# First expert layer's head: four buffers for scales, separate PSUM banks, another order on GpSimd and VectorE

## The reference, cut to what matters

```python
x = x + _L0_xattn_ref(_layernorm(x), ctx_1024, ctx_1024, ...)
x = x + _L0_ffn_ref(_layernorm(x), ...)          # below; its x is the normalised one
...
def _L0_ffn_ref(x, g1, be1, mix_w, mix_b, g2, be2, router_w, w1, b1, w2, b2):
    res = x
    n = layer_norm(x, g1, be1)
    x = res + n + (n @ mix_w + mix_b)
    res = x
    n = layer_norm(x, g2, be2)
    probs = softmax(flat @ router_w)              # flat: n as 4096 x 128
    topw, topi = top_k(probs, 2)
    h = silu(einsum('td,edf->tef', flat, w1) + b1)
    y = einsum('tef,efd->ted', h, w2) + b2
    return res + einsum('te,ted->td', combine, y) # combine: topw at the two chosen experts
```

## Time and profile before

| what | value |
|---|---|
| median of 3 runs | 1463.12 us (1462.66 to 1466.3) |
| profiled execution, its own time | 1462.91 us |
| span of the profiled execution | 1461.1 us |
| busy: PE / DVE / ACT / POOL | 80% / 68% / 46% / 37% of the span |
| attention of layer 0 ends | at 223.2 us |
| head of the first expert layer | 223.2 to 322.6 us |
| units of the first expert layer | 322.6 to about 510 us |

### The profile page before, as it was taken

How to read it: one execution, slowest core, us unless ns; L and a number is a source line. 1 busy time by engine, 2 the same in 40 slices (tenths; PEclk the granted TensorE clock), 3 DMA queues, 4 the chain that set the end, 5 groups by cost and what they waited for, 6 DMA issues and landing times. The chain is left out here.

```text
span 1461.1 us, 34924 instructions
## 1 busy us (share of the span) xinstructions
PE 1174.6 (80%) x11141; PEld 920.6 (63%) x11154; DVE 987.4 (68%) x2918; ACT 667.0 (46%) x1423; POOL 538.6 (37%) x590
## 2 busy tenths in 40 slices
PE   4799994349999957789987879999799856499991
PEld 2577773238899825566673456667477655399991
DVE  4689886554533248988984678888487777766552
ACT  2467771115555403445564546666233343144440
POOL 3223303674324166534411242431121125652564
PEclk9999995559999957889998989999799988599996
DMA  7887733012223267435532177564200042133542
GB/s 181 205 217 192 184 93 129 30 56 75 82 91 108 66 158 188 116 101 150 144 84 51 52 170 177 144 160 106 87 1 0 6 147 76 53 120 107 147 144 70
DMA packets 140294, 163.33 MB, mean 112 GB/s; under 512 B 15240, under 2 KB 120734, under 8 KB 133196
## 3 DMA queue, kind: packets, MB, share of 16 engines
q1 hardware_dynamic: 131980, 145.38, 37.0%
q0 software_dynamic: 8192, 16.46, 4.0%
HBM read 111.19 MB, written 50.92 MB: 111 GB/s over the span
## 5 line engine op out<-in xcount | busy, mean ns | idle before, releaser
L604 DVE TENSOR_REDUCE A_neg_max<-A_s_bank 128x4 f32<-128x512 f32 x384 | 254.0, 688 | 54.3 <-PE A_s_bank L747 43.9
L464 ACT ACTIVATE A_probsT<-A_st_bank 128x512 f32<-128x512 f32 x384 | 222.3, 602 | 50.1 <-PE A_st_bank L760 48.7
L747 PE MATMUL A_s_bank<-A_k_stack,A_q_stack 72*128 72x128 bf16 x1536 | 159.0, 230 | 42.5 <-DMA A_q_stack<-q_scratch 22.3
L760 PE MATMUL A_st_bank<-A_q_stack,A_k_stack 128*128 128x128 bf16 x1536 | 153.6, 225 | 7.2 <-DVE A_q_stack L620 6.4
L760 PEld LDWEIGHTS A_st_bank<-A_q_stack,A_k_stack 128*128 128x128 bf16 x1536 | 113.0, 104 | 53.5 <-issue 43.5
L747 PEld LDWEIGHTS A_s_bank<-A_k_stack,A_q_stack 72*128 72x128 bf16 x1536 | 107.2, 102 | 57.3 <-DVE A_neg_max L604 30.0
L772 PE MATMUL A_pv_bank<-A_probsT,A_v_pad 128*32 128x128 f32 x3072 | 127.5, 284 | 1.0 <-issue 1.0
L2065 ACT ACTIVATE E_h<-E_h_bank,w_L_b 128x256 f32<-128x256 f32 x184 | 76.8, 471 | 73.2 <-PE E_h_bank L2165 72.1
L2177 PE MATMUL E_y_bank<-E_w,E_h 128*128 x736 | 90.3, 276 | 2.2 <-ACT E_h L2065 0.9
L2165 PE MATMUL E_h_bank<-E_xT,E_w_u 128*128 128x256 f32 x368 | 89.5, 388 | 0.0
L772 PEld LDWEIGHTS A_pv_bank<-A_probsT,A_v_pad 128*32 128x32 f32 x3072 | 74.2, 111 | 24.2 <-issue 2.7
(11 more groups left out here) (369 smaller groups left out, 2639.7 us busy)
## 6 DMA issues: line engine op xcount, KB each, us to landing
A_q_stack<-q_scratch SPq DMA_DIRECT2D x48, 576.0 KB
A_k_stack<-k_scratch SPq DMA_DIRECT2D x32, 576.0 KB
q_scratch<-A_q_parts SPq DMA_DIRECT2D x48, 192.0 KB
A_k_stack<-k_scratch SPq DMA_DIRECT2D x48, 192.0 KB
E_xe<-slots_in SPq DMA_DIRECT2D x53, 128.0 KB, 2.1
slots_out<-E_ye SPq DMA_DIRECT2D x53, 128.0 KB
A_ctxT<-in_ctxT SPq DMA_DIRECT2D x24, 256.0 KB, 9.3
k_scratch<-A_k_parts SPq DMA_DIRECT2D x32, 192.0 KB
```

Source lines behind the costliest of these rows:

```text
L464: act.activation(probsT[n % 2][:, c * HQ:(c + 1) * HQ, :], st_bank[c % 2][:, :].rearrange("k (a q) -> k a q", a=HQ), ACT.Exp, scale=scale) ...
L604: dve.tensor_reduce(neg_max[:, c * HQ:(c + 1) * HQ], s_bank[c % 2][:, :].rearrange("q (a k) -> q a k", a=HQ), AX.X, ALU.max, negate=True). ...
L747: last = pe.matmul(s_bank[c % 2][:, a * S:(a + 1) * S], q_stack[slot][0:COMBO, h, at:at + S], k_stack[slot][0:COMBO, h, at:at + S], start= ...
L760: last = pe.matmul(dst, k_stack[slot][:, h, at:at + S], q_stack[slot][:, h, at:at + S], start=True, stop=spread)
```

## The change

1. `scale_z`, `rstd_x` and `back` get four buffers (`NR = 4`) where they had two.
2. Banks of the head: `mix` of odd groups goes to `h_bank[0]`, `turn_r` to `x_bank` and `y_bank`, logits and counts to `h_bank[1]`. These banks belong to the units, which begin later; PE gets three waits in unit 0 for it. With that, `mix` waits for `z_added` of two groups before, `turn_z` for `n_copied`, and PE's `mix` of a new chunk no longer waits for `index_done`.
3. GpSimd's list: all four `scale_of_z` stand before the first scatter, and `inverse_deviation(1)` and `(2)` come after 4 scatters of chunk 0 and 8 of chunk 1.
4. VectorE's list: `scale(0)` and `scale(1)` come before the conversion of the bias `mix_b`; `statistics` of the groups 2 and 3 before the first `mix`, of 4 and 5 before `normalise` of chunk 0, of 6 and 7 after it; `normalise` before `add_x1`; both `scale` of the next chunk before `below_max`.
5. `convert_rest` is no block any more: its five conversions are in VectorE's list of the expert layer before the first `mix`, and its barrier is gone.

```diff
-        scale_z = [sb(f"scale_z{i}", [S, RT]) for i in range(2)]
+        scale_z = [sb(f"scale_z{i}", [S, RT]) for i in range(NR)]
...
-        l_bank = m_bank
+        in_head = lambda g: g < 2 * HEAD
+        mixed_bank = lambda g: h_bank[0] if in_head(g) and g % 2 else m_bank
+        rows_bank = lambda g: (x_bank, y_bank)[g % 2] if in_head(g) else t_bank[g % 2]
+        logit_bank = lambda c: h_bank[1] if c < HEAD else m_bank
...
             pool.memset(zeros[:, :], 0.0).then_inc(zeroed, 1)
             scale_of_z(0)
+            scale_of_z(1)
             inverse_deviation(0)
-            scale_of_z(1)
+            scale_of_z(2)
+            scale_of_z(3)
             pool.wait_ge(cleared, 16 * len(PARTS))
-            scatter(0, 0, 8)
+            scatter(0, 0, 4)
             inverse_deviation(1)
-            scatter(0, 8, 2 * RT)
-            scale_of_z(2)
-            scatter(1, 0, 10)
+            scatter(0, 4, 2 * RT)
+            scatter(1, 0, 8)
             inverse_deviation(2)
-            scatter(1, 10, 2 * RT)
-            scale_of_z(3)
+            scatter(1, 8, 2 * RT)
...
+            scale(0)
+            scale(1)
             dve.wait_ge(mix_b_loaded, 48)
...
-            scale(0)
-            scale(1)
+            statistics(2)
+            statistics(3)
+            convert(dve, own)
             for c in range(HEAD):
                 for g in (2 * c, 2 * c + 1):
                     mix(g)
                     statistics_1(g)
+                if c == 0:
+                    statistics(4)
+                    statistics(5)
+                normalise(2 * c)
+                normalise(2 * c + 1)
                 add_x1(2 * c)
                 add_x1(2 * c + 1)
-                statistics(2 * c + 2)
-                normalise(2 * c)
-                normalise(2 * c + 1)
-                statistics(2 * c + 3)
-                below_max(c)
+                if c == 0:
+                    statistics(6)
+                    statistics(7)
                 if c + 1 < HEAD:
                     scale(2 * c + 2)
+                    scale(2 * c + 3)
+                below_max(c)
                 choose_first(c)
                 choose_second(c)
-                if c + 1 < HEAD:
-                    scale(2 * c + 3)
                 locate(c)
...
             def mix(g):
                 if g == 0:
                     pe.wait_ge(mix_done, 2)
-                else:
-                    pe.wait_ge(z_added, g)
-                if g % 2 == 0 and g >= 2:
-                    pe.wait_ge(index_done, g // 2)
+                elif g >= 2:
+                    pe.wait_ge(z_added, g - 1 if in_head(g) else g)
...
                 if c + 1 < HEAD:
                     turn_z(2 * c + 2)
+                    turn_z(2 * c + 3)
+                    mix(2 * c + 2)
                 count(c)
                 if c + 1 < HEAD:
-                    turn_z(2 * c + 3)
-                    mix(2 * c + 2)
                     mix(2 * c + 3)
```

More of the change, by code:

```diff
@@ L1566, in routed_ffn @@
         mv_x = sb("mv_x", [S, NB, 2])
-        scale_z = [sb(f"scale_z{i}", [S, RT]) for i in range(2)]
-        rstd_x = [sb(f"rstd_x{i}", [S, RT]) for i in range(2)]
-        back = [sb(f"back{i}", [S, RT]) for i in range(2)]
+        scale_z = [sb(f"scale_z{i}", [S, RT]) for i in range(NR)]
+        rstd_x = [sb(f"rstd_x{i}", [S, RT]) for i in range(NR)]
+        back = [sb(f"back{i}", [S, RT]) for i in range(NR)]
         z = sb("z", [S, RT, D])
@@ L2042, in copy_r @@
                     act.wait_ge(l_ready, g - 1)
-                act.activation(rT[g % 2][:, :], t_bank[g % 2][:, :], ACT.Identity, scale=g2[:, 0:1], bias=be2[:, 0:1])\
+                act.activation(rT[g % 2][:, :], rows_bank(g)[:, :], ACT.Identity, scale=g2[:, 0:1], bias=be2[:, 0:1])\
                     .then_inc(r_copied, 1)
@@ L2124, in turn_r @@
                 pe.wait_ge(r_done, g + 1)
-                pe.wait_ge(n_copied, g + 1)
+                if not in_head(g):
+                    pe.wait_ge(n_copied, g + 1)
+                elif g >= 2:
+                    pe.wait_ge(r_copied, g - 1)
                 for j in range(GB):
-                    last = pe.transpose(t_bank[g % 2][:, j * S:(j + 1) * S], r[:, g * GB + j, :], core.ident[:, :])
+                    last = pe.transpose(rows_bank(g)[:, j * S:(j + 1) * S], r[:, g * GB + j, :], core.ident[:, :])
                 last.then_inc(r_turned, 1)
@@ L2131, in logits @@
                 pe.wait_ge(r_copied, g + 1)
-                pe.wait_ge(z_added, (g | 1) + 1)
+                if not in_head(g):
+                    pe.wait_ge(z_added, (g | 1) + 1)
+                elif g >= 2:
+                    pe.wait_ge(index_done, g // 2)
                 for j in range(GB):
                     i = g % 2 * GB + j
-                    last = pe.matmul(l_bank[:, i * NE:(i + 1) * NE], rT[g % 2][:, j * S:(j + 1) * S], router_w,
+                    last = pe.matmul(logit_bank(g // 2)[:, i * NE:(i + 1) * NE], rT[g % 2][:, j * S:(j + 1) * S], router_w,
                                      start=True, stop=True)
@@ L2152, in turn_slots @@
                     pe.wait_ge(x_copied, u)
+                else:
+                    pe.wait_ge(r_copied, 2 * HEAD)
                 for j in range(2):
@@ L2973, in load_expert, with convert_rest @@
             sp.dma_start(exp_w1[:, at], ap["L0_exp_w1"].rearrange("d e f -> d (e f)")[:, at]).then_inc(exp_w1_loaded, 16)
-        def convert_rest():
-            with nc.Block() as block:
-                @block.vector
-                def _(dve):
-                    dve.wait_ge(rest_loaded, 16 * len(rest_loads))
-                    dve.tensor_copy(core.earlier[:, :], wide_earlier[:, :])
-                    dve.tensor_copy(core.first_tie[:, :], wide_first_tie[:, :])
-                    dve.tensor_copy(q_w2, q_w2f, saturate=False)
-                    dve.tensor_copy(q_b2h, q_b2f).then_inc(quantised, 1)
-                    dve.wait_ge(quantised, 1)
-                    dve.tensor_copy(q_b2, q_b2h)
+        def convert_rest(dve, own):
+            dve.wait_ge(rest_loaded, 16 * len(rest_loads))
+            own.did(dve.tensor_copy(core.earlier[:, :], wide_earlier[:, :]))
+            own.did(dve.tensor_copy(core.first_tie[:, :], wide_first_tie[:, :]))
+            own.did(dve.tensor_copy(q_w2, q_w2f, saturate=False))
+            own.link(dve.tensor_copy(q_b2h, q_b2f))
+            own.did(dve.tensor_copy(q_b2, q_b2h))
         if 0 in stages:
```

38 lines of the change are left out of this document (20 added, 18 removed).

## The result

| what | before | after |
|---|---|---|
| median of 4 runs each, side by side | 1464.71 us (1462.66 to 1468.12) | 1450.13 us (1447.66 to 1455.78) |
| ratio after / before, 95% interval | | 0.9919 (0.9895 to 0.9944) |
| profiled execution, its own time | 1462.91 us | 1452.55 us |
| VectorE's first instruction behind the attention | 224.19 | 222.67 |
| SP's first load of a unit | 320.52 | 306.90 |

The change is faster by 0.8%, which is 11.9 us of 1464.7 (8.2 to 15.4). The forecast of 1452.2 lies 0.4 from the profiled execution and 2.1 from the median. The head, as the table measures it, is 12.10 shorter where 10.8 was predicted. It is measured from the first instruction behind the attention, because the attention itself, which is the same code, ended 1.52 earlier in this execution.

The account below looks back on a forecast made before the run. GpSimd's scatters, held up mutually with VectorE, bound the units' start. Shorter waits bring the first load from 320.52 to 309.7, gain 10.8: 1462.91 - 10.8 = 1452.1, said 1452.2 us; own range 1451 to 1454, with rivals 1449.5 to 1456.5.

Parts of the forecast that it names:

- Barrier and conversions: Start of the expert layer: it begins 1.40 us earlier, but five conversions on VectorE delay the first mix by about 1.05.
- The banks: Head, chunks 0 and 1: a second bank removes the 1.14 us wait; chunk 1's mixes no longer wait for the index.
- then 2.81: GpSimd, after its wait for chunk 2's mixes: inverse_deviation(2) takes 2.81 us, before the last eight scatters.
- Eight scatters: GpSimd, after the deviation of chunk 2: the last eight scatters take 10.06 us and end at 307.1.
- From the last scatter's end to the load: End of the head: the last scatter's landing and the issue take 2.6 us, so the first load comes at 309.7.
- The remaining wait: GpSimd, before the deviation of chunk 2: it waits 1.7 us for VectorE's mixes, behind table(0) and three weight copies.
- The first rival: GpSimd slower beside VectorE's denser list, scatters 1.29 us each, deviations 2.81: gain 8.6, time 1454.3 us; chance 0.16.
- the prediction's sign of 1.3: GpSimd in the head: the prediction is wrong if scatters without pauses take over 1.3 us each.
- the second rival: No wait before chunk 2's deviation, which takes 2.22 us: 2.3 more gain, time 1449.8 us; chance 0.09.
- Scales that come late: GpSimd's scales not ahead in fact: VectorE's delay past 1.5 and 3.9 us of room delays scatters; about 1455.5; chance 0.06.
- a loss at unit 23: Units begin 10.8 us earlier, but PE stands at unit 23 for the second part's scatters: no change, 1462.9; chance 0.05.
- a lower clock in the units: TensorE's clock stays at the head's lower level; four units at it cost 16.4 us, time 1468.5; chance 0.04.

Follow-up runs that it names:

- the two halves of the list: Two kernels, each the changed one with half of GpSimd's new list: scales ahead, deviations late, head 87.05 us; deviations early, scales between, head 96.87 us.
- the experiment on it: The changed kernel with add_x1 put back ahead of normalise: head 85.52 us, ratio to the kernel before 0.9928.

## Why the prediction was right

- **The mechanism.** The forecast said that GpSimd and VectorE hold each other up through GpSimd's list. Putting back the list alone gave back 10.2 of 12.1 and the time of before, and the two halves of the list show that the scales are what matters. The list is needed, but is not enough: with the old banks and the block it brings 6.1.
- **Barrier and conversions.** A net gain of 0.35 was predicted (1.40 less 1.05). With the block put back the first mix is 0.37 later, as predicted, but the 32nd scatter is not: the sum carried this gain through to the load, and there it is not. That the head differs by 0.33 all the same, by the stretch behind the scatters, is luck. The conversions taken off the path brought the first mix 1.02 sooner and gave 0.91.
- **The banks.** The prediction needed them twice, for chunk 0's wait and for chunk 1's mixes that no longer wait for the index, and did not price them apart: 5.2 with the new lists, TensorE's order included.
- **Sizes that were off.** The head is 1.28 shorter than predicted (84.23 for 85.51), in four terms. The deviation of chunk 2 starts 69.33 after the layer's beginning, predicted 70.0 (294.2 less 224.19): 0.7, nearly all of it from the steps up to index 0, where VectorE's 34 instructions from normalise to the scale took 7.62 (242.92 to 250.54) and not the 7.99 that adding up their lengths gave, and normalise came 0.26 sooner. The deviation took 2.19 and not 2.81: 0.62. The step "then 2.81" took its price from a row in which add_x1 ran beside it; this change moves add_x1 away, as the experiment on it shows. The same price stands in chunk 0, as 2.65 on VectorE; there it was 2.25 (240.67 to 242.92), which is why normalise came sooner. So about 1.0 of the 1.28 is this one price. Eight scatters took 10.36 for 10.06, 0.3 the other way, since one of them now meets add_x1. From the last scatter's end to the load were 2.35 for 2.6; that goes with the block, as said, and its cause is open.
- **The remaining wait.** Predicted 1.7, measured 1.09. Index 0 was 0.65 sooner for both engines, but GpSimd's twenty scatters took 25.76 where the prediction has 25.2, so that only VectorE was 0.7 sooner at the deviation, and GpSimd 0.1. Its cause, the table and the weight copies, is shown by the kernel in which they stand behind the mixes: no wait, head 1.03 less.
- **The rivals.** The first rival came true in one half: the twenty scatters took 1.29 each and the last eight 1.30, the pace it names and the edge of the prediction's sign of 1.3, against 1.26 in the sum, 0.9 in all. The wait for VectorE hid 0.6 of it, and the other half, deviations of 2.81, did not come (2.21 and 2.19). The evidence against this rival, scatters that kept their pace beside VectorE's work in the old trace, was weak: those that met add_x1 there happened not to be drawn out (last section). Of the second rival too one half came: the deviation took 2.19, for its 2.22, but 1.09 of the wait stayed. Scales that come late, a loss at unit 23, a lower clock in the units: the rows show none of them.
- **The time.** That the profiled execution took 1452.55, 0.4 from the forecast, is luck: the head gained 1.3 more than predicted, the attention ended 1.5 sooner, and the stages behind took 3.1 more. The median, 1450.13, lies in the range of 1449.5 to 1456.5 but outside the forecast's own 1451 to 1454, and nearest to the second rival's 1449.8. Four runs between 1447.66 and 1455.78 can't tell these two apart; the wait of 1.09 in the rows does.

## What to carry to other kernels

An engine with a hand-written list holds up all who wait for anything in it: look for short steps on which another engine waits that stand behind a long run of steps nobody waits for yet, and move the inputs of these steps early enough. The pieces are not additive: early deviations were worth 2.8 with early scales and cost 2.5 without, and the banks, with TensorE's order, were worth 5.2 with GpSimd's new list, while with its old one banks, VectorE's order and the missing block together were worth 1.9. When a price is read from a row, read what ran beside it as well, since the change may move just that. And when a difference has the size that was predicted, follow it along the chain: the 0.33 of the block didn't come by the predicted way.

## What the runs showed of the hardware

Some of GpSimd's instructions are drawn out where they meet add_x1, the one step of VectorE here that reads two float32 operands of 128x512 from SBUF (1.26 to 1.29 us for two). A scatter takes 1.32 or 1.33 for 0.96, a power 1.95 for 1.67, a step of 0.24 takes 0.58 ahead of a deviation, and up to 1.18 in a scale at 245.16 in the changed kernel, where add_x1 runs from 244.94:

```profile
244.94 1.29 DVE L1822 TENSOR_TENSOR x_sb<-x_sb,E_x 128x512 f32<-128x512 f32 x2
...
245.16 1.18 POOL L1722 TENSOR_SCALAR E_roots<-E_mv_x 128x8 f32<-128x8 f32 x1
246.42 1.66 POOL L1723 TENSOR_TENSOR E_rstd_x<-E_roots,minus_half 128x8 f32<-128x8 f32 x1
```

That step ends at 246.34, 0.11 behind add_x1: it looks held until the addition is through. The Trainium skill (SBUF — State Buffer, section "Who interferes with whom") says that a VectorE instruction with two SBUF inputs contends with a GpSimd instruction that reads SBUF; the rows agree, and put the price at 0.3 to 0.9 us for each meeting that drew a step out. Where a step begins seems to count: the scatter that began at 266.62, 0.47 ahead of an add_x1, and ran on beside it kept its 0.96, while the next one, begun within it, took 1.32. In the trace of before, add_x1 ran from 268.20 to 269.46, and two scatters of chunk 0 met it; one began 0.14 ahead of it, one 0.14 before its end, and neither was drawn out:

```profile
268.06 0.96 POOL L1739 DMA_INDIRECT routed_in<-E_r,E_index  x1 [0.31 <-issue]
269.32 0.97 POOL L1739 DMA_INDIRECT routed_in<-E_r,E_index  x1 [0.30 <-issue]
```

No run here tells that apart further.
